# A decoder layer on one core: the next sequence's queries and keys are made in front of the later scores by key

## The reference

```
x = layernorm(x + self_attention(x, w_qkv, b_qkv, w_proj, b_proj))      # causal, 16 heads of 16
x = layernorm(x + cross_attention(x, ctx, w_q, w_k, w_v, w_o))           # 16 heads of 64, 77 keys
h = concat([x, -x]);  h = 2 * relu(s0 * (h @ K0));  h = 2 * relu(s1 * (h @ K1))
x = layernorm(x + s2 * (h @ K2))                                         # K0, K1, K2 hold +1 or -1
```

## Time and profile before

| | us |
|---|---|
| median of 3 runs | 2594.97 |
| lowest and highest | 2594.3, 2595.82 |
| the profiled execution, its own time | 2596.83 |
| its span in the profile | 2594.7 |
| one pass of the loop (from 1243.99 to 1315.52) | 71.5 |

### The profile page before, as it was taken

The page is one execution under the profiler, slowest core; times in us unless marked ns, Lnnn a source line. Parts: engine busy times, 40 slices in busy tenths (PEclk is TensorE's granted clock), DMA queues, the critical chain, the costliest instruction groups (busy, mean ns, idle before and its releaser), DMA issues.

```text
span 2594.7 us, 54039 instructions
## 1 busy us (share of the span) xinstructions
PE 2208.4 (85%) x18572; PEld 1910.5 (74%) x18572; DVE 1570.9 (61%) x4804; ACT 1013.4 (39%) x1800; POOL 688.5 (27%) x847
## 2 busy tenths in 40 slices
PE   7995578988888888898888888888988888888897
PEld 6884467877777777787777777777877777777776
DVE  4542356666666666676666666666666666666664
ACT  5552234433334333444333333434433334333442
POOL 1000223232223222322323232233233223222321
PEclk9997689999999999999999999999999999999999
DMA  8885333223323333322332333333223323333310
GB/s 268 278 276 143 62 62 67 50 53 59 60 40 65 65 65 65 65 56 53 54 61 47 55 65 65 65 65 62 54 52 61 61 38 65 65 65 65 65 37 9
DMA packets 205155, 196.57 MB, mean 76 GB/s; under 512 B 50130, under 2 KB 184306, under 8 KB 205042
## 3 DMA queue, kind: packets, MB, share of 16 engines
q1 hardware_dynamic: 205108, 195.94, 36.5%
HBM read 69.37 MB, written 58.87 MB: 49 GB/s over the span
## 4 chain that ended last, share of the span: by engine, by line
PE 57%; DVE 14%; DMA 11%; issue 9%; SPq 5%; ACT 3%; DVEq 1%; POOL 0%; POOLq 0%
DMA k_bd<-p2t 9%; PE ps L1149 9%; PE ps L1318 8%; PE ps L1172 4%; PE ps L1189 4%; PE ps L1190 4%; PE ps L1225 4%; PE ps L1238 4%; PE ps L1286 3%; SPq L393 3%; PE ps L1130 2%; DVE junk L821 2%; PE ps L1138 2%; DVE max L860 2%; PE ps L1214 2%
## 5 line engine op out<-in xcount | busy, mean ns | idle before, releaser
L1189 PE MATMUL ps<-r_h,w 128*128 128x256 f16 x2048 | 497.7, 285 | 2.3 <-DVE r_l L807 2.3
L1190 PE MATMUL ps<-r_l,w 128*128 128x256 f16 x2048 | 494.0, 284 | 0.0
L821 DVE CUSTOM_DVE_ANT_0 junk<-ps,causal 128x128 bf16<-128x128 f32 (+1 forms) x1024 | 328.9, 355 | 154.8 <-PE ps L1214 151.2
L490 POOL TENSOR_TENSOR p<-p2r,inv 128x308 f32<-128x308 f32 x256 | 199.2, 778 | 584.6 <-DVE inv L879 584.6
L1213 PE MATMUL ps<-k_bd,q_st 128*128 128x256 f32 x256 | 95.2, 372 | 227.5 <-DMA k_bd<-p2t 203.4
L476 POOL TENSOR_SCALAR_AFFINE_SELECT probs<-probs 128x512 f32<-128x512 f32 x256 | 164.0, 641 | 375.8 <-ACT probs L621 372.5
L565 ACT ACTIVATE r_h<-ps 128x512 f16<-128x512 f32 x256 | 152.6, 596 | 276.0 <-PE ps L1190 268.4
L1318 PE MATMUL ps<-vo_h,p2t 128*128 128x256 f32 (+1 forms) x1280 | 234.9, 290 | 28.7 <-DVE p2t L886 27.6
L807 DVE SCALAR_TENSOR_TENSOR r_l<-ps,r_h 128x512 f16<-128x512 f32 x256 | 176.1, 688 | 132.7 <-ACT r_h L565 132.7
L1189 PEld LDWEIGHTS ps<-r_h,w 128*128 128x128 f16 x2048 | 209.8, 102 | 38.3 <-issue 4.7
L1213 PEld LDWEIGHTS ps<-k_bd,q_st 128*128 128x128 f32 x256 | 52.4, 205 | 249.4 <-DMA k_bd<-p2t 180.9
(11 more groups left out here) (146 smaller groups left out, 5164.3 us busy)
## 6 DMA issues: line engine op xcount, KB each, us to landing
vo_scratch<-vo_out SPq DMA_DIRECT2D x80, 448.0 KB, 4.4
vo<-vo_scratch SPq DMA_DIRECT2D x64, 512.0 KB
q_st<-p2t SPq DMA_DIRECT2D x192, 128.0 KB
k_bd<-p2t SPq DMA_DIRECT2D x192, 128.0 KB, 6.7
q<-q SPq DMA_DIRECT2D x128, 128.0 KB, 2.1
k_bd<-k_scratch SPq DMA_DIRECT2D x64, 154.0 KB, 3.5
x_in<-in_x SPq DMA_DIRECT2D x32, 256.0 KB, 5.5
out<-y SPq DMA_DIRECT2D x32, 256.0 KB, 6.8
```

What stands on the lines that cost most here:

```text
L490: pool.tensor_tensor(unit_probs(t), raw, inv.unsqueeze(3).to_broadcast([P, TB, 2, SK]), ALU.mult)\
L821: dve.tensor_tensor_reduce(out=junk[:, e, b * P:b * P + width], in0=ps[:, 2 + b, e * width:(e + 1) * width], in1=causal[:, (1 - b) * P:], ...
L1189: pe.matmul(dst, w1[:, kk, m * P:(m + 1) * P], r0_h[:, kk, :], start=kk == 0, stop=False)
L1190: last = pe.matmul(dst, w1[:, kk, m * P:(m + 1) * P], r0_l[:, kk, :], start=False, stop=kk == KF - 1)
```

## The change

The transposes of x, the queries and the keys of sequence i + 1 move ahead on every engine: the transposes behind `transposed_max(i, 1)`, the queries in front of score by key 4, the keys between scores 6 and 7. All of them, and the values, now use bank 3, one after the other, with waits for the bank's readers. The outputs of both halves of the heads share bank 2. `head_stacks` is split: the queries' DMAs stand between the two packed outputs, behind a wait for the last score by key, and the keys' behind the second packed output. x is loaded at the head of the pass. In cross-attention steps of layer 1 move behind the transposes, and the row maximum of pair 3 stands one unit later.

```diff
@@ SP
-            def head_stacks(j):
+            def query_stacks(j):
+                if not (isinstance(j, int) and j == 0):
+                    sp.wait_ge(pe_st, nth(j, NP, 0))
                 sp.wait_ge(a_qk, nth(j, 4, 2))
...
+            def key_stacks(j):
                 sp.wait_ge(a_qk, nth(j, 4, 4))
...
             def attention(i, g, first=False, more=True):
+                if more:
+                    load(i + 1)
...
-                if more:
-                    load(i + 1)
                 stack_max(i, 1)
...
-                if more:
-                    head_stacks(i + 1)
+                output_packed(i, 0)
+                if more:
+                    query_stacks(i + 1)
+                output_packed(i, 1)
+                if more:
+                    key_stacks(i + 1)
@@ ScalarE (attention)
                 self_probs(i, 3)
+                if more:
+                    transposed_x(i + 1)
...
                 self_probs(i, 4)
+                if more:
+                    queries_keys(i + 1, 0)
                 self_probs(i, 5)
                 self_output(i, 0)
                 self_probs(i, 6)
+                if more:
+                    queries_keys(i + 1, 1)
+                self_probs(i, 7)
                 if not first:
                     relu(0, r0_h, pe_z0, a_r0, f, 0)
-                self_probs(i, 7)
-                if more:
-                    transposed_x(i + 1)
                 self_output(i, 1)
...
@@ VectorE (attention)
                     ffn_sum(g, 0)
-                if not first:
-                    transposed_x2(f)
+                if more:
+                    transposed_x(i + 1)
                 if g is not None:
                     ffn_sum(g, 1)
+                if not first:
+                    transposed_x2(f)
+                if more:
+                    queries_keys(i + 1, 0)
+                    queries_keys(i + 1, 1)
+                if g is not None:
                     layer_norm_stats(2, y3, g)
+                if more:
+                    queries_keys(i + 1, 2)
+                    queries_keys(i + 1, 3)
...
                 layer_norm_apply(0, x1, x1, d_x1, i)
+                if more:
+                    self_max(i + 1, 0)
                 dve.wait_ge(a_x1t, nth(i, 1, 1))
...
-                if more:
-                    self_max(i + 1, 0)
...
-                    if t in (2, 4) and more:
-                        self_max(i + 1, 1 + t // 2)
+                    if t in (2, 5) and more:
+                        self_max(i + 1, 2 + t // 4)
@@ PE
+                if g == 2:
+                    pe.wait_ge(a_o, nth(i, 2, 1))
...
             def queries_keys(j, u):
+                if u == 0:
+                    pe.wait_ge(a_xt, nth(j, 1, 1))
+                    pe.wait_ge(d_xt, nth(j, 1, 1))
+                else:
+                    pe.wait_ge(d_qk, nth(j, 4, 2))
...
             def self_values(j):
+                pe.wait_ge(d_qk, nth(j, 4, 4))
...
                 cross_scores(i, 6)
-                layer1_until(f, 17, 18)
                 cross_scores(i, 7)
-                layer1_until(f, 18, 19)
                 cross_transposes(i, 0, 0)
                 cross_transposes(i, 0, 1)
-                layer1_until(f, 19, 22)
+                layer1_until(f, 17, 20)
...
-                layer1_until(f, 22, 24)
+                layer1_until(f, 20, 24)
```

More of the change, by code:

```diff
@@ L413, in attention @@
                 load_value_outputs(i)
+                stack_max(i, 1)
+                output_packed(i, 0)
                 if more:
-                    load(i + 1)
[L416 to L421, removed]
+                    query_stacks(i + 1)
+                output_packed(i, 1)
                 if more:
-                    head_stacks(i + 1)
+                    key_stacks(i + 1)
                 if g is not None:
@@ L432, in store @@
                   .then_inc(stored, 16)
-            head_stacks(0)
+            query_stacks(0)
+            key_stacks(0)
             stack_max(0, 0)
@@ L828, in transposed_x @@
                 dve.wait_ge(a_xt, nth(j, 1, 1))
-                dve.tensor_tensor(xt_l[:].rearrange("p a b -> p (a b)"), ps[:, 4, :],
+                dve.tensor_tensor(xt_l[:].rearrange("p a b -> p (a b)"), ps[:, 3, :],
                                   xt_h[:].rearrange("p a b -> p (a b)").bitcast(F32), ALU.subtract).then_inc(d_xt, 1)
@@ L916, in attention @@
                 if more:
-                    for m in range(4):
-                        queries_keys(i + 1, m)
                     self_values(i + 1)
@@ L1237, in values @@
                         src = pr[:, (2 * g + j // 2) % 4, j % 2, (1 - b) * P:(3 - 2 * b) * P]
-                        last = pe.matmul(ps[32 * j:32 * j + 32, 2 + g // 2, c + b * P:c + S], v[:, b, 4 * g + j, :], src,
+                        last = pe.matmul(ps[32 * j:32 * j + 32, 2, c + b * P:c + S], v[:, b, 4 * g + j, :], src,
                                          start=b == 0, stop=b == 1)
@@ L1244, in transposed_inputs @@
                 pe.wait_ge(x_loaded, nth(j, 16, 16))
-                transposes(x_in, 4, j, pe_xt)
+                transposes(x_in, 3, j, pe_xt)
             def queries_keys(j, u):
+                if u == 0:
[3 more added lines that the diff above has]
+                    pe.wait_ge(d_qk, nth(j, 4, 2))
                 for m in (2 * u, 2 * u + 1):
-                    last = weights_by_tokens(ps[:, 6 + m // 2, (m % 2) * S:(m % 2 + 1) * S], wqkv_h, wqkv_l,
+                    last = weights_by_tokens(ps[:, 3, (m % 2) * S:(m % 2 + 1) * S], wqkv_h, wqkv_l,
                                              slice(m * P, (m + 1) * P), xt_h, xt_l)
@@ L1255, in self_values @@
             def self_values(j):
+                pe.wait_ge(d_qk, nth(j, 4, 4))
                 for b in range(TB):
-                    last = tokens_by_weights(ps[:, 5, b * D:(b + 1) * D], xt_h, xt_l, b, wqkv_h, wqkv_l,
+                    last = tokens_by_weights(ps[:, 3, b * D:(b + 1) * D], xt_h, xt_l, b, wqkv_h, wqkv_l,
                                              slice(2 * D, 3 * D))
@@ L1365, in attention @@
                 scores_by_key(i, 6)
+                if more:
+                    queries_keys(i + 1, 1)
+                scores_by_key(i, 7)
                 filler0(1)
-                scores_by_key(i, 7)
                 values(i, 2)
-                if more:
-                    pe.wait_ge(a_p, nth(i, NP, NP - 1))
-                    transposed_inputs(i + 1)
                 if g is not None:
@@ L1379, in attention @@
                 filler0(5)
-                if more:
-                    pe.wait_ge(a_xt, nth(i + 1, 1, 1))
-                    pe.wait_ge(d_xt, nth(i + 1, 1, 1))
-                    queries_keys(i + 1, 0)
                 filler0(6)
@@ L1406, in attention @@
                 pe.wait_ge(k2_loaded, nth(i, 32, 32))
-                if more:
-                    pe.wait_ge(d_qk, nth(i + 1, 4, 4))
-                    pe.wait_ge(d_v, nth(i + 1, 1, 1))
                 def next_scores(n):
@@ L1475, in _ @@
             self_values(0)
+            pe.wait_ge(d_v, 1)
             pe.wait_ge(q_stacked, 112)
```

26 lines of the change are left out of this document (13 added, 13 removed).

## The result

| | us |
|---|---|
| before, median of 4 | 2594.99 |
| after, median of 4 (2524.51 to 2529.46) | 2528.41 |
| ratio, with its 95% interval | 0.9741 (0.9724 to 0.9757) |
| after, the profiled execution and its span | 2524.51, 2522.5 |
| one pass, mean of 26 in the loop: before, after | 71.7, 69.6 |

What follows compares the result with a forecast made beforehand. PE's query score waiting for the key stacks, with half clock behind, was taken to bound the kernel; 0.5 + 1.9 - 1.5 + 0.75 = 1.65 us for each of 29 sequences, 57 us with the rest, gave 2538, range 2450 to 2600.

Steps and rivals of the forecast that it cites:

- Step 1: Queries and keys made early: QK1 shares bank 3 with QK0, so PE stands 0.7 us.
- Steps 2 and 3: Tail of layer 0, PE standing 1.5 us before step 6; packed outputs, PE standing 3.9 us before layer 1's fourth step.
- step 3: Packed outputs: second pair served in turn behind six query stacks; 5.6 of 6.1 us of wait given back, gain 0.5.
- Step 4: Clock: 1.9 us gained at the query score, 1.5 given back by the 3.9 us stop; bounds nothing or the whole 1.9.
- Step 5: Cross region: first cross output starts 0.85 us earlier, 0.75 kept at the end; bounds 0 and 0.85.
- the 9 us for what lies outside the 29 passes: Gains outside sequences 2 to 30: sequence 0 gives 5 us, sequence 1 gives 3, the last 0.7.
- Rival (a): The clock holds through the 3.9 us stop: 100 us gained, 2495 us; chance 0.24.
- Rival (b): Second packed pair not held up, landing near t = 14: 5.0 us per sequence, 2441 us; chance 0.13.
- Rival (c): Query stacks slower beside other work, delaying the packed pair; decides at 1.34 us each, 2632 us at 1.6; chance 0.15.
- Rival (d): Wait only moves: cross region gives nothing, stops 0.9 us longer; within 0.2% of the old time, 2595 us; chance 0.08.

Runs made afterwards that it cites:

- the kernel with two queues: Changed kernel with the second packed pair issued by ScalarE on its own DMA queue, SyncE issuing the stacks without it: 2451.80 us, ratio to before 0.9447.
- the split kernel: Changed kernel with the second packed pair issued behind four of the six query stacks, the two low ones following it: 2429.95 us, ratio to before 0.9369.

## Why the prediction was right, point by point

2538 was forecast and 2528 measured. The case named likeliest is the one that occurred: the key wait goes, PE stops three times instead, and the clock falls in the third stop. Term by term, per pass:

| | forecast | measured |
|---|---|---|
| wait taken away | 6.1 | 5.7 to 6.3, 6.0 in the mean |
| wait for bank 3 | 0.7 | 0.35 |
| layer 0, step 6 | 1.5 | 1.1 |
| layer 1, fourth step | 3.9 | 3.3 to 3.65 |
| first stack's issue to use of the pair | 9.1 | 8.6 to 9.0 |
| clock, taken away and given back | 1.9 - 1.5 | 1.9 - 1.9 |
| cross region | 0.75 | 1.0 |
| sum of the gains | 1.65 | 2.04 |

- Step 1, right with its place, half its size. VectorE's low parts let PE go on at t = 4.75, just as forecast (1186.13, with t counted from 1181.38, where the queries begin behind the transposes of x2); but PE comes to this wait at t = 4.4, not 4.05.
- Steps 2 and 3, right. Step 6 of layer 0 is released at t = 12.0 (forecast 12.05), and PE comes to it at 10.9, not 10.5. The first stack is issued at 7.6, as forecast, and the pair is used at 16.3, not 16.7. The stops came to 4.9 us instead of 6.1; that is the largest mis-sized term, and by it the gain was understated.
- The sum of step 3 has a slip: stops of 0.7, 1.5 and 3.9 are 6.1 us, no less than the wait that went, and the 0.5 by which they were made 5.6 is no gain but work of PE counted short, since the text itself calls the work of the region the same. In the traces it is the same, 20.5 us at full clock in both. So 0.5 was forecast here where the forecast's own stops give 0, and 1.1 (6.0 - 4.9) was measured.
- Step 3's reason, that the pair is served in turn in SP's queue, was wrong as the whole reason. It gave the right landing, because the stacks in flight set it, and the pair on another queue showed that. The Trainium skill, "DMA: Bandwidth & Descriptors", section "Queues, rings and completion order", gives SP and ScalarE a ring each on the same 16 engines, which take the rings in turn by packet. The packets of the kernel with two queues agree from the pair's first one on (256 KB of it and 205 KB of stacks in the same 3.2 us); but that the pair would then land soon does not follow, since 297 KB of stacks run before its first packet.
- Step 4, right in kind, with the sum too favourable: of 1.9 us of clock per pass (the idle matmuls on the kernel before) the same 1.9 came back (the idle matmuls on the changed one), so nothing that these runs can tell was left where 0.4 was forecast. The bound "the whole 1.9" was the right one.
- Step 5, right in its chain, undersized by 0.25 us. The first cross output starts 9.2 us behind the last group of cross queries in the kernel with this part alone and 10.2 us behind it before, so the whole 1.0 is there already, where 0.85 was worked out and 0.75 kept.
- Of the 9 us for what lies outside the 29 passes, 66.6 - 59 = 7.6 appeared.
- That the time came within 10 us of the forecast is in part luck: the slip of 0.5 and the 0.4 of clock were too favourable, the stops (1.2) and the cross region (0.25) not enough, and most of it cancels.

Rival (a), the clock holding, did not occur in the changed kernel, but did with a stop of 1.5 us. Rival (b), a pair that is not held up, is out: even on its own queue it was. Rival (c), slower stacks, needed 1.34 us a stack; four and six stacks ahead of the pair differ by 2.0 us in the median (6.75 and 8.7 from the first issue to the use), 1.0 each. Rival (d) would have had longer stops and no gain in the cross region.

## What to carry to other kernels

A wait of PE for a transfer was traded here for a wait further up the same chain, because the earlier transfer now stood in the way of a smaller one that is needed sooner; asking of each transfer that is moved ahead which small one it overtakes found the cost beforehand, and moving two of six stacks behind the pair gave 98 us more, against 67 for the whole change. What a stop of PE costs behind it, by the clock, goes with its length: here stops of 1.5 us cost nothing (the split kernel), those of 1.8 to 2.4 us let the clock fall in some passes (8 of 30 and 12 of 30), and those of 3.3 us and more in every one. Before real work is moved into a stop, look at what it covered where it came from. And where every pass has a fall of the clock in it, a small gain elsewhere can be taken back by it; try it on a kernel whose clock holds.

## What the runs showed of the hardware that was not expected

- A 128 KB transfer within SBUF that takes 2.1 us alone took 5.1 us from issue to use with stacks in flight, though it was on another engine's queue; in the stacks' own queue it took 4.7 behind six of them, and 3.8 when issued at the same moment as in the 5.1 us case, with the rest of the stacks behind it. A queue of its own gave no priority.
- The clock's price for one and the same stop differs from pass to pass: stops of 3.3 to 3.65 us left the following stretch at 7.4, 7.7 or 8.7 to 9.0 us, where it is 6.2 with the clock at 1.00.
- A loop can keep its length against a gain. With a wait of about 6 us in each pass, the falls of the clock followed each other by 71.7 us in the kernel before and, but for three places, in the one with 1.0 us less work per pass. The mean granted clock in the wait went from 0.75 to 0.93 and behind it from 0.61 to 0.50 (windows of one pass each), and 0.6 us of the 1.0 was lost in the loop. Two edits' gains therefore need not add up: the same one was worth 17, 31 and 32 us.
